# Attention products of a windowed transformer stack on TensorE: contraction over 64 keys in two row halves of the array, instead of over 128 keys with zero halves in the values

## What is computed

```python
w = WINDOW                                   # 32 tokens, 16 heads of 64
bq, bk, bv = (t.reshape(b, h, nw, w, d) for t in (q, k, v))
look = ...                                   # each window sees its own 32 keys and the 32 before
sim = jnp.einsum('bhwie,bhwje->bhwij', bq, look(bk)) * QK_SCALE
attn = jax.nn.softmax(where(mask, -max, sim), -1)
out = jnp.einsum('bhwij,bhwje->bhwie', attn, look(bv))
```

## Time and profile before

| | us |
|---|---|
| median of three runs | 3814.31 |
| profiled execution: span from its first to its last instruction | 3806.1 |
| TensorE busy (PE) | 3546.5, 93% |
| its weight loads (PEld), beside the matmuls | 2001.1, 53% |
| VectorE busy (DVE) | 3233.6, 85% |
| ScalarE busy (ACT) | 2526.1, 66% |
| GpSimd busy (POOL) | 1558.0, 41% |
| products, L1053, two groups | 327.7 and 324.1 |
| scores, L1041 | 296.2 |
| ScalarE's copies into va, L945 and L946 | 192.5 and 193.7 |

### The profile page before, as it was taken

How to read it: one execution, slowest core, us unless ns; L and a number is a source line. 1 busy time by engine, 2 the same in 40 slices (tenths; PEclk the granted TensorE clock), 3 DMA queues, 4 the chain that set the end, 5 groups by cost and what they waited for, 6 DMA issues and landing times. The chain is left out here.

```text
span 3806.1 us, 123350 instructions
## 1 busy us (share of the span) xinstructions
PE 3546.5 (93%) x51360; PEld 2001.1 (53%) x51360; DVE 3233.6 (85%) x3696; ACT 2526.1 (66%) x3409; POOL 1558.0 (41%) x926
## 2 busy tenths in 40 slices
PE   5999879899999999999999999999999999999997
PEld 2333245555555555555555555555555555555554
DVE  7999778788888888888888888888888889888895
ACT  4888757667666666666766667667666666666764
POOL 4333144344434444434444434344444434444341
PEclk7999989999999999999999999999999999999999
DMA  2000011111121111121111111111211111211112
GB/s 69 2 1 1 23 44 34 28 27 34 29 61 34 27 34 28 37 58 27 34 28 34 50 38 34 28 29 38 55 34 29 27 40 27 62 29 27 37 30 62
DMA packets 60833, 130.63 MB, mean 34 GB/s; under 512 B 16004, under 2 KB 31880, under 8 KB 60424
## 3 DMA queue, kind: packets, MB, share of 16 engines
q1 hardware_dynamic: 60424, 124.06, 13.4%
HBM read 23.58 MB, written 4.19 MB: 7 GB/s over the span
## 5 line engine op out<-in xcount | busy, mean ns | idle before, releaser
L798 POOL TENSOR_TENSOR half_sq<-sq 128x1024 f32<-128x1024 f32 x192 | 500.9, 2609 | 1541.9 <-ACT sq L933 1531.9
L1072 PE MATMUL slot<-w_qkv,xs 128*128 (+1 forms) x2304 | 1102.7, 608 | 25.6 <-issue 17.3
L803 POOL TENSOR_TENSOR cosq<-cosq,sinq 128x1024 f32<-128x1024 f32 x384 | 902.2, 2366 | 368.7 <-DVE sinq L843 368.7
L933 ACT ACTIVATE sq<-slot 128x1024 f32<-128x1024 f32 x384 | 392.0, 1021 | 405.3 <-PE slot L1072 405.3
L1072 PEld LDWEIGHTS slot<-w_qkv,xs 128*128 128x128 f32 x2304 | 411.2, 192 | 432.2 <-issue 423.5
L841 DVE TENSOR_TENSOR cosq<-slot,table 128x1024 f32<-128x1024 f32 x384 | 467.7, 1218 | 143.4 <-ACT sq L933 133.1
L869 DVE TENSOR_TENSOR qk<-cosq,ry 128x1024 f32<-128x1024 f32 x384 | 517.8, 1359 | 11.6 <-ACT ry L990 9.5
L843 DVE TENSOR_TENSOR sinq<-slot,table 128x1024 f32<-128x1024 f32 x384 | 465.8, 1213 | 0.0
L1023 PEld LDWEIGHTS slot<-ident,qk 128*128 128x128 f32 x3072 | 349.5, 141 | 215.0 <-issue 125.3
L1023 PE MATMUL slot<-ident,qk 128*128 128x128 f32 x3072 | 396.1, 275 | 36.4 <-DVE qk L869 32.2
L1053 PE MATMUL slot<-vb,probT 128*32 128x130 f32 x6144 | 327.7, 280 | 16.9 <-issue 10.6
(11 more groups left out here) (123 smaller groups left out, 4940.6 us busy)
## 6 DMA issues: line engine op xcount, KB each, us to landing
vb<-va SPq DMA_DIRECT2D x720, 130.0 KB, 2.3
w_qkv<-in_w_qkv SPq DMA_DIRECT2D x21, 512.0 KB, 5.3
w_o<-in_w_o SPq DMA_DIRECT2D x6, 512.0 KB
w<-in_w SPq DMA_DIRECT2D x6, 342.0 KB
res<-in_x SPq DMA_DIRECT2D x4, 512.0 KB, 5.3
out<-w_qkv SPq DMA_DIRECT2D x8, 256.0 KB, 3.2
kept<-res SPq DMA_DIRECT2D x1, 1536.0 KB, 6.2
w<-in_w SPq DMA_DIRECT2D x6, 171.0 KB
```

The costliest lines, as they stand in the source:

```text
L798: nc.gpsimd.tensor_tensor(half_sq[:, :, :], squares[:, :, 0, :], squares[:, :, 1, :], ALU.add).then_inc(S["folded"], 1)
L803: nc.gpsimd.tensor_tensor(cosq[:, side], cosq[:, side], sinq[:, side], ALU.add).then_inc(S["qk"[side] + "_added"], 1)
L933: nc.scalar.activation(sq[:, "qk".index(name)].rearrange("p h d -> p (h d)"), flat(name, n), ACT.Square).then_inc(S[name + "_squared"], 1)
L1072: last = nc.tensor.matmul(slot(kind, n)[:, i, :], xs[:, n * P:(n + 1) * P], w_qkv[:, (0 if layer is None else layer) % 2, "qkv".index(kind ...
```

## The change

`va` and `vb` lose their second axis and the zero halves: a tile's 128 tokens stand in one 65-wide entry per head. ScalarE fills `va` with one copy of 128 partitions. One DMA shifts 96 partitions, a second takes the 32 of the tile before; tile 0 has one, the others two. The products contract over 64 keys: for each window pair there are two matmuls, b = 0 in the lower and b = 1 in the upper 64 rows, each with 65 streamed columns, into PSUM bank b. A kind has 32 matmuls instead of 16. The PSUM layout is now bank b, then position x = 2 n + r, and VectorE's two instructions read it in that order. GpSimd clears half as much and writes the ones in one instruction per tensor.

```diff
--- before.py
+++ after.py
@@ -62,8 +62,8 @@
         self.xs = sb("xs", [P, SEQ])
         self.xs2 = sb("xs2", [P, SEQ])
         self.kT = [sb(f"kT{i}", [P, QCH, WIN + P]) for i in range(2)]
-        self.va = sb("va", [P, VTILES, 2, HEADS, VA])
-        self.vb = sb("vb", [P, VTILES, 2, HEADS, VA])
+        self.va = sb("va", [P, VTILES, HEADS, VA])
+        self.vb = sb("vb", [P, VTILES, HEADS, VA])
         self.S = {n: sem("ws_" + n) for n in ("const_loaded", "const_ready", "w_q", "w_k", "w_v", "qks_loaded", "w_ff",
                                               "cleared", "mask_loaded", "kept", "fetched")}
 
@@ -132,14 +132,13 @@
                                   (early.minus_least, -1e-24), (early.xs, 0.0), (early.xs2, 0.0)):
                 pool.memset(buffer[:, :], value).then_inc(cleared, 1)
             for v in (early.va, early.vb):
-                pool.memset(v[:, :, :, :, :], 0.0).then_inc(cleared, 1)
+                pool.memset(v[:, :, :, :], 0.0).then_inc(cleared, 1)
             pool.wait_ge(cleared, 11)
             pool.wait_ge(loaded, 32)
             nc.gpsimd.tensor_tensor(early.centring[:, :], ident[:, :], early.ones[:, :], ALU.subtract).then_inc(cleared, 1)
             pool.wait_ge(cleared, 12)
             for v in (early.va, early.vb):
-                pool.memset(v[0:DH, :, 0, :, DH:VA], 1.0).then_inc(ready, 1)
-                pool.memset(v[DH:P, :, 1, :, DH:VA], 1.0).then_inc(ready, 1)
+                pool.memset(v[:, :, :, DH:VA], 1.0).then_inc(ready, 1)
 
         @block.vector
         def _(dve):
@@ -686,9 +685,9 @@
                                                         "rstd_link", "passed"]}
         S.update(early.S)
         vb_ready = [sem(f"ws_vb_ready{t}") for t in range(TPB)]
-        VB_DMAS = [3] + [4] * (TPB - 1)
+        VB_DMAS = [1] + [2] * (TPB - 1)
         W_FF = 5
-        CONSTS = 7
+        CONSTS = 5
         block = ctx.enter_context(nc.Block())
 
         wait = event_wait(S, EVENTS)
@@ -772,11 +771,9 @@
 
                 s = t % VTILES
                 wait(sp, "v_read", unit, t)
-                sp.dma_start(vb[32:64, s, 0, :, :], va[0:32, s, 0, :, :]).then_inc(vb_ready[t], 16)
-                sp.dma_start(vb[64:96, s, 1, :, :], va[32:64, s, 0, :, :]).then_inc(vb_ready[t], 16)
-                sp.dma_start(vb[96:128, s, 1, :, :], va[64:96, s, 1, :, :]).then_inc(vb_ready[t], 16)
+                sp.dma_start(vb[32:128, s, :, :], va[0:96, s, :, :]).then_inc(vb_ready[t], 16)
                 if t:
-                    sp.dma_start(vb[0:32, s, 0, :, :], va[96:128, (t - 1) % VTILES, 1, :, :]).then_inc(vb_ready[t], 16)
+                    sp.dma_start(vb[0:32, s, :, :], va[96:128, (t - 1) % VTILES, :, :]).then_inc(vb_ready[t], 16)
             units(sp, SP_ORDER, stage, layer_end)
 
             for name in ("w_q", "w_k", "w_v", "qks_loaded"):
@@ -882,9 +879,9 @@
                     wait(dve, kind + "_filled", unit, n)
 
                     wait_tile(dve, "turned", unit, n)
-                    ps = slot(kind, n)[:, :, 0:4 * PITCH].rearrange("p r (w d) -> p r w d", d=PITCH)
+                    ps = slot(kind, n)[:, :, 0:4 * PITCH].rearrange("p b (x d) -> p b x d", d=PITCH)
                     link(nc.vector.reciprocal(rden[:, a], ps[:, :, :, DH]), kind)
-                    nc.vector.tensor_tensor(o[:, a].rearrange("p w r d -> p r w d"), ps[:, :, :, 0:DH],
+                    nc.vector.tensor_tensor(o[:, a].rearrange("p (b w) r d -> p b (w r) d", b=2), ps[:, :, :, 0:DH],
                                             rden[:, a, :, :, None].broadcast_to([P, 2, 4, DH]), ALU.mult).then_inc(S[kind + "_read"], 1)
                 elif kind == "turn":
 
@@ -942,8 +939,7 @@
                         wait_vb(act, unit_of, old + 1)
                     wait(act, "v_filled", unit, n)
                     ps = flat("v", n).rearrange("p (h d) -> p h d", d=DH)
-                    nc.scalar.copy(va[0:DH, n % VTILES, 0, :, 0:DH], ps[0:DH])
-                    nc.scalar.copy(va[DH:P, n % VTILES, 1, :, 0:DH], ps[DH:P]).then_inc(S["v_read"], 1)
+                    nc.scalar.copy(va[:, n % VTILES, :, 0:DH], ps).then_inc(S["v_read"], 1)
                 elif kind == "qT":
                     wait(act, "qT_filled", unit, n)
 
@@ -1046,16 +1042,18 @@
 
             def products(kind, t):
                 a = ("va", "vb").index(kind)
-                for r in range(2):
-                    for n, values in enumerate((vb, va)):
+                for n, values in enumerate((vb, va)):
+                    for r in range(2):
+                        at = (2 * n + r) * PITCH
                         for g in range(4):
-
-                            last = nc.tensor.matmul(
-                                slot(kind, t)[32 * g:32 * g + 32, r, 0:4 * PITCH].rearrange("p (w d) -> p w d", d=PITCH)[
-                                    :, n::2, 0:VA],
-                                probT[:, 4 * r + 2 * a + n, 32 * g:32 * g + 32],
-                                values[:, t % VTILES, :, 2 * (4 * a + g) + r, :],
-                                start=True, stop=True, skip_group_check=True)
+                            for b in range(2):
+                                keys = slice(DH * b, DH * b + DH)
+
+                                last = nc.tensor.matmul(
+                                    slot(kind, t)[32 * g:32 * g + 32, b, at:at + VA],
+                                    probT[keys, 4 * r + 2 * a + n, 32 * g:32 * g + 32],
+                                    values[keys, t % VTILES, 2 * (4 * a + g) + r, :],
+                                    start=True, stop=True, skip_group_check=True)
                 return last
 
             def stage(kind, n, unit, batch, before, starts, layer):
```

## The result

The changed kernel takes 3891.98 us (median of 4 runs, 3882.09 to 3896.05) against 3814.26 of the kernel before in the same session: ratio 1.0202, 95% interval 1.0188 to 1.0215. It is 2.0% slower, by 78 us, and lies above the predicted range.

A forecast was written before the change was run, and what follows sets the result against it. TensorE was taken to bound the kernel. A span of 3806.1 us, less 71 of cashed matmul gain, plus 67 of instruction stalls, gave 3802, with launch 3810 us; own range 3780 to 3840, 8 in 10 range 3750 to 3865.

The forecast's parts named there:

- What bounds: TensorE sets the pace in the windowed stack, busy 95.5%; its issue stalls of 47.3 and 25.2 us must be understood.
- The matmuls: Products va and vb: lone kinds from 1.03 to 0.78 us, pairs from 1.91 to 1.42, gaining 95 us.
- Not cashed: At kT0's wait for scaled k and s0's for va3's reading, 12 us each of the gain becomes wait, leaving 71.
- The price of a block: TensorE's 256-instruction blocks take 3.0 us each (2.7 to 3.3); added stalls, mainly in vb2, vb1, s0, cost net 67 us.
- rival (2): Slower: a block takes 3.5 us or more when blocks follow closely or meet vb transfers; 3860 us, chance 17%.
- The loop's head: A 0.95 us stall at a unit's head was left unpriced; the stall after 122 records of s3 was to stay.
- The rest: ScalarE's copies lose 192 us, nothing off the end; DMAs, VectorE's normalising and GpSimd's clearing add 0; packets near 490.
- Rival (1): TensorE's instruction fetch hides and the gain is cashed: 3743 us, up to 3760 with a few stalls; chance 22%.

The follow-up runs named there:

- e5: The changed kernel with TensorE's loop body moved on by half a block (128 instructions): 3938.0 us, ratio 1.0325.
- e2: The changed kernel with the old value path put back (two copies of 64 partitions, three shifts plus the carry): 3912.4 us, ratio 1.0231.
- e7: The kernel before with each unit of the loop body beginning 32 instructions into a block: 3764.4 us, ratio 0.9873.
- e1: The kernel before with each product of 130 columns cut into two of 65: 3947.4 us, ratio 1.0326.

## Why the prediction was wrong

**What bounds: right.** TensorE; and the two issue rows were the place to look.

**The matmuls: right within a fifth.** Lone kinds 0.79 for 0.78. Pairs 1.56 for 1.42: the first 32 records take 0.26 us (8 ns each), the later halves 0.51, and the gain a unit is 4 x 0.24 + 2 x 0.35 = 1.7 us where I had 1.98; 80 us in all where I had 95. The rate of the scores row was near the right one, 64 records in 0.79 us being 12 ns each with the changeover. The Trainium skill's 60 cycles a matmul (TensorEngine Tiling (Array Packing), Instruction Overhead) are not borne out by these rows.

**Not cashed: smaller than said.** The wait for scaled k stayed at 32.2 us, and s0's for VectorE's reading of va3 went from 8.0 to 9.5 us (0.17 to 0.27 each, in 36 places for 47). I had 24 us of new waits and took 30 us of them and of the old away again where a stall would take their place: -6 us in all, measured +2. Single waits for k read as predicted, 1.40 us where no stall precedes (at 1323.99, 1.5 predicted) and none where one does (at 1181.05, behind the stall of 1.48).

**The price of a block: the step that failed.** "I take 3.0, and 2.7 and 3.3 as ends of a mean." The eleven blocks that follow each other without slow work take 3.57 to 4.11 us, 3.77 in the mean (3.84 from 1471.10 to 1474.94 and from 1192.48 to 1196.32). I had three places, none a block wholly filled by short records, counted their start by instructions from the stop before, and took the mean of all stalls in place of the rows of 1.18 us, which gave 3.4 for both. I had 8.1 us of added stalls in a loop body, 97 in all; the issue idle alone grew by 119, to which come some 0.2 us each for 86 more stops that hide under the last record's tail: about 136. This is rival (2), with its place and sign: at 3.77 its own sum, ten ends x 0.77 x 12 = 92, less the same sixth, gives 3810 + 77 = 3887. That this is so near the result is partly luck: it makes 97 + 92 = 189 us of gross stalls, more than were found, and leaves out the next point.

**A term that was missing: the clock.** Neither forecast nor rival had a price for the clock. From 745 us on the line of the q/k/v tiles is busy 1033.2 us against 1006.1, 27 more with the same work, nearly all of it in groups at the low clock. It reaches other work too: the score stage after 1192.82 takes 1.80 us for 108 records in place of 1.32. Ledger of the span, measured: products -69, scores +8 (tails at stops), issue +119, q/k/v +27, sum 85 of +86. And what the forecast of -4 us missed by 90: block price and number of stalls 39 (136 for 97), clock 27, products 15 (80 for 95), waits 8, sum 89.

**The loop's head: misplaced, little harm.** I took the stop after 122 records of s3 as fixed behind the branch. The head is at the q0 of every fourth unit (1310.20, eight records, 1.58 us of idle), the one row that I "couldn't price", which the align line puts at a block's start. I left it as it was; its ten stops sum to 9.6 us before and 14.2 after. e5, which moves the head, moves every stop.

**The rest: right.** ScalarE 194 us down, VectorE unchanged, value path free (e2), 489 packets for 490.

**Rival (1)** and the sentence of the Trainium skill (Runtime: NRT & Kernel Launch, Instruction fetch mechanics) that a crossing is mostly hidden: true of most blocks with slow work in them, as e7 with 33 us of issue idle in all; not of blocks made of some 128 short records, which run in 1.7 us against some 3.8 from crossing to crossing.

## What to carry to other kernels

Count instructions as well as columns: where TensorE's program is unrolled as here, a block of 256 has to last some 3.8 us (4.0 in one block that still stood 0.29), and short matmuls with their loads use it up in 1.7. Replacing one instruction by two shorter ones paid here only in the forms where slower work stood in the same blocks. Before cutting work, see which stalls are called "issue", count to the next one, and try moving where the blocks end: an alignment and two moved tiles were worth 69 us at the end in the kernel before, as much as the products' whole saving in busy time.

## What was not expected of the hardware

- The next block seems not to be asked for at the crossing. The packet of 1189.5 starts some 0.5 us after the first record of its pair of products (1188.98, behind a q/k/v tile), with no transfer in the window before it. A request made only once the sequencer is some way into a block, which it can't be while it waits, fits this and guided the offset of 32; no run tests it by itself.
- The granted clock can fall to its lower level for some us after stalls at issue of 1.5 to 2 us (0.50 in the window of 1193.9). It did so after 25 of the 56 stalls of 1.5 us or more, and not after the others, in one case at the same two records with stalls no shorter (2032.89 and 2036.73).
- Products in two row halves: 64 x 65 records start every 8 to 9 ns in the first half of a kind and every 16 ns in the second (0.27 and 0.51 us for 32 records); e1's 128 x 65 records take 0.23 us for 16, as 8 of 128 x 130 take 0.22: they cost by the column, and the two row halves are what saves.
